# Attention exps: two of each group's 32 leave ScalarE for VectorE and GpSimd

## The reference, cut to what matters

```python
q = _rms_norm(q)
k = _rms_norm(k)
attn = jnp.einsum('bhnd,bhmd->bhnm', q, k) * scale      # scale = D ** -0.5 = 0.25
attn = jax.nn.softmax(attn, axis=-1)
y = jnp.einsum('bhnm,bhmd->bhnd', attn, v)
```

## Time and profile before

| what | us |
|---|---|
| median of 3 runs | 810.57 (808.7 to 810.73) |
| the profiled execution | 810.5 |
| its span, first to last instruction | 808.7 |
| PE busy | 781.2 (97%) |
| DVE busy | 476.2 (59%) |
| ACT busy | 523.3 (65%) |
| POOL busy | 245.1 (30%) |

### The profile page before, as it was taken

One profiled execution on the slowest core, in us unless ns is written; L12 is line 12 of the kernel. 1 busy time (PEld: TensorE's weight loads), 2 busy tenths in 40 slices (PEclk: granted clock), 3 DMA queues, 4 the chain that ended last, 5 costly groups with the idle time before them and its releaser, 6 DMA issues.

```text
span 808.7 us, 13174 instructions
## 1 busy us (share of the span) xinstructions
PE 781.2 (97%) x4440; PEld 514.7 (64%) x4440; DVE 476.2 (59%) x855; ACT 523.3 (65%) x699; POOL 245.1 (30%) x310
## 2 busy tenths in 40 slices
PE   8999999998999999999999999999999999999994
PEld 5778888886777887433332332332756788888884
DVE  5887676557866762382321211220467699999994
ACT  4432222463233226899999999999465688888883
POOL 6434444223434421500000000100000376656652
PEclk9999999999999999999999999999996999999999
DMA  8141111101132805043453432400682581111000
GB/s 247 34 80 53 41 37 52 53 1 53 42 119 100 180 2 79 1 73 109 81 143 41 79 52 28 80 1 1 219 303 104 197 303 48 56 47 43 24 12 0
DMA packets 52762, 64.99 MB, mean 80 GB/s; under 512 B 15969, under 2 KB 44009, under 8 KB 52716
## 3 DMA queue, kind: packets, MB, share of 16 engines
q1 hardware_dynamic: 44580, 55.96, 26.7%
q0 software_dynamic: 3312, 6.31, 2.5%
q10 hardware_dynamic: 4824, 2.12, 1.0%
HBM read 51.52 MB, written 15.60 MB: 83 GB/s over the span
## 4 chain that ended last, share of the span: by engine, by line
PE 83%; DVE 9%; ACT 3%; issue 2%; DMA 1%; DVEq 0%; ACTq 0%; POOLq 0%; SPq 0%
PE psum L1656 46%; PE psum L1761 15%; PE psum L1748 12%; PE psum L2033 2%; PE psum L1847 2%; DVE hl L1078 1%; DVE hh L1226 1%; PE psum L1719 1%; PE psum L1911 1%; DVE ssum L1266 1%; DMA x_tm<-in_x 1%; DVE w_lo L1527 1%; DVE parts L1335 1%; DVE parts L1334 1%; DVE qk_tm L1298 1%
## 5 line engine op out<-in xcount | busy, mean ns | idle before, releaser
L845 ACT ACTIVATE pexp<-psum 128x1024 f32<-128x1024 f32 x256 | 238.0, 1124 | 5.2 <-PE psum L1748 4.3
L832 ACT ACTIVATE hid<-psum,b_col 128x512 f32<-128x512 f32 x96 | 66.1, 689 | 164.1 <-PE psum L1656 124.1
L1761 PE MATMUL psum<-pexp,v_ones 128*32 128x512 f32 x1024 | 136.0, 604 | 0.0
L1748 PEld LDWEIGHTS psum<-q_stack,k_stack 48*128 48x128 f32 x512 | 44.3, 183 | 124.2 <-ACT pexp L845 105.2
L1748 PE MATMUL psum<-q_stack,k_stack 48*128 48x512 f32 x512 | 109.4, 476 | 2.9 <-DVE parts L1335 2.9
L1226 DVE TENSOR_SCALAR hh<-hid,scale_col 128x341 fp32r<-128x341 f32 x192 | 71.0, 411 | 61.6 <-ACT hid L832 44.4
L1078 DVE SCALAR_TENSOR_TENSOR hl<-hid,scale_col,hh 128x341 fp32r<-128x341 f32 x192 | 104.6, 586 | 3.4
L1349 DVE COPY yT<-psum 128x512 f32<-128x512 f32 x16 | 11.0, 691 | 131.4 <-PE psum L1761 131.4
L1656 PE MATMUL psum<-hh,w2h 128*128 128x512 f32 x192 | 76.8, 400 | 3.9 <-DVE hl L1078 3.8
L1656 PE MATMUL psum<-x_hi,w1h 128*128 128x512 f32 x192 | 77.4, 403 | 0.6 <-DVE x_lo L1092 0.5
L1656 PE MATMUL psum<-hh,w2l 128*128 128x512 f32 x192 | 75.4, 393 | 0.0
(11 more groups left out here) (284 smaller groups left out, 1438.0 us busy)
## 6 DMA issues: line engine op xcount, KB each, us to landing
w_all<-in_L_ffn_W SPq DMA_DIRECT2D x16, 1024.0 KB, 7.4
raw<-in_L_cond_ew SPq DMA_DIRECT2D x32, 256.0 KB, 3.3
parts_d<-parts SPq DMA_DIRECT2D x8, 1024.0 KB, 4.1
q_stack<-parts_d SPq DMA_DIRECT2D x48, 128.0 KB, 4.2
k_stack<-parts_d SPq DMA_DIRECT2D x48, 128.0 KB, 6.6
raw<-in_L_cond_sw SPq DMA_DIRECT2D x16, 256.0 KB, 3.4
x_tm<-in_x SPq DMA_DIRECT2D x4, 512.0 KB, 7.3
x_d<-x_tm SPq DMA_DIRECT2D x2, 1024.0 KB, 10.4
```

The lines of the kernel that those rows point to most:

```text
L832: act.activation(hid[k % 4][:], bank(k % 4), ACT.Gelu_apprx_tanh, bias=b1_col[:, bass.ds(4 * q + k // 2, 1)]).then_inc(gelu_done, 1)
L845: act.activation(pexp[mt % 2][:, 2 * j:2 * j + 2, 512 * h:512 * h + 512], psum[:, 2 * r:2 * r + 2, :], ACT.Exp, scale=D ** -0.5)\
L1748: ins = pe.matmul(psum[:, 2 * r + lane, :], k_stack[i][rows, j, mt * P:(mt + 1) * P], q_stack[i][rows, j, 512 * h:512 * h + 512], start=Tr ...
L1761: ins = pe.matmul(psum[VW * j:VW * j + VW, 6 + h, :], v_ones[i][:, mt, j, :], pexp[mt % 2][:, j, 512 * h:512 * h + 512], start=(mt == 0), ...
```

## The change: what it does

Units 12 and 20 of groups 1 to 7 (14 of 256 units) take another way. VectorE copies their scores from PSUM into the place in `pexp` where their exps belong. GpSimd then replaces them by `exp_base ** score`, where `exp_base` holds e to the power of 0.25, so that the result is the same exp. TensorE's `slot_free` waits for VectorE's copy where the pair held such a unit, and `values` waits for GpSimd's count beside ScalarE's. ScalarE skips these units. VectorE's loops over the groups are written out, and `split_parts` now stands in the order of the units, between the copies.

```diff
+POOL_EXPS = [(g, u) for g in range(1, 8) for u in (12, 20)]
...
+        def other_exps(n):
+            return sum(1 for g, u in POOL_EXPS if UNITS * g + u < n)
+
+        def exps_until(eng, n):
+
+            eng.wait_ge(exp_done, n - other_exps(n))
+            after(eng, pool_exp_done, other_exps(n))
...
+            pool.memset(exp_base[:], math.exp(D ** -0.5)).then_inc(exp_base_made, 1)
...
+            def exp_unit(g, u):
+
+                mt, h, j = u // HG, u % HG // 2, u % 2
+                unit = pexp[mt % 2][:, 2 * j:2 * j + 2, 512 * h:512 * h + 512]
+                pool.wait_ge(score_copied, other_exps(UNITS * g + u + 1))
+                pool.tensor_tensor(unit, exp_base[:].unsqueeze(2).to_broadcast([P, 2, 512]), unit, ALU.pow)\
+                    .then_inc(pool_exp_done, 1)
...
+                for u in range(UNITS):
+                    if g and (g, u) in POOL_EXPS:
+                        exp_unit(g, u)
...
-                if u % 2 == 0:
+                if u % 2 == 0 or (g, u - 1) in POOL_EXPS:
                     after(act, av_done, 2 * LT * g + u // 2 - 3)
...
-                    exp_unit(g, u)
+                    if (g, u) not in POOL_EXPS:
+                        exp_unit(g, u)
...
+            def copy_scores(g, u):
+
+                mt, h, j = u // HG, u % HG // 2, u % 2
+                r = pair(("scores", g, u))
+                dve.wait_ge(scored, UNITS * g + u + 1)
+                after(dve, av_done, 2 * LT * g + u // 2 - 3)
+                dve.tensor_copy(pexp[mt % 2][:, 2 * j:2 * j + 2, 512 * h:512 * h + 512],
+                                psum[:, 2 * r:2 * r + 2, :]).then_inc(score_copied, 1)
+
+            for g in range(GROUPS - 1):
+                take_output(g)
+                finish_group(g // (H // HG), g % (H // HG))
+                for u in range(UNITS):
+                    if (g + 1, u) in POOL_EXPS:
+                        copy_scores(g + 1, u)
+                    if (g + 1, u) in QK_AT:
+                        split_parts(QK_AT.index((g + 1, u)))
...
-                if what == "scores":
-                    pe.wait_ge(exp_done, UNITS * g + u + 1)
+                if what == "scores" and (g, u) in POOL_EXPS:
+                    pe.wait_ge(score_copied, other_exps(UNITS * g + u + 1))
+                elif what == "scores":
+                    pe.wait_ge(exp_done, UNITS * g + u + 1 - other_exps(UNITS * g + u))
...
-                pe.wait_ge(exp_done, UNITS * g + 2 * v + 2)
+                exps_until(pe, UNITS * g + 2 * v + 2)
```

More of the change, by code:

```diff
@@ L15 @@
+import math
 from contextlib import ExitStack
@@ L130, in layer_kernel @@
         ones = sb("ones", [P, P], F32)
+        exp_base = sb("exp_base", [P, 1], F32)
         scan_keep = sb("scan_keep", [P, RE, TT], F32)
@@ L348, in layer_kernel @@
         exp_done = sem("exp_done")
+        pool_exp_done = sem("pool_exp_done")
+        exp_base_made = sem("exp_base_made")
+        score_copied = sem("score_copied")
         av_done = sem("av_done")
@@ L700, in _ @@
                 pool.memset(v_ones[i][:, :, :, D:D + 1], 1.0).then_inc(v_base, 1)
+            def exp_unit(g, u):
[4 more added lines that the diff above has]
+                    .then_inc(pool_exp_done, 1)
+            pool.wait_ge(exp_base_made, 1)
             for g in range(GROUPS):
@@ L1833, in turn_ctx @@
                 if w == 0:
-                    pe.wait_ge(exp_done, UNITS * GROUPS)
+                    exps_until(pe, UNITS * GROUPS)
                 pe.wait_ge(ctx_done, 4 if w < 4 else 8)
```

## The result

| | median us | range of the runs | ratio to before |
|---|---|---|---|
| before | 810.57 | 808.7 to 810.73 | |
| changed | 3057.46 | 3056.78 to 3058.91 | 3.774 (3.766 to 3.783) |

The kernel is 2246.9 us slower. The forecast of 804.7 us was wrong, and the time lies far outside the range that ended at 865 us.

The account below looks back on a forecast made before the run. ScalarE's exps were taken to bound attention, with TensorE's floor next. Five groups gaining 1.2 us each, groups 1 and 2 almost nothing, gave 810.6 - 5.9 = 804.7 us, range 802.5 to 865.

Parts of the forecast that it names:

- the price of the power on GpSimd: A 128x1024 power on GpSimd was taken as under 3.5 us, from the 1.89 us product of the same shape.
- The upper bound: Longest GpSimd power considered: 14 arithmetic passes of 1.89 us, 26.5 us, making the kernel 316 us slower.
- The first rival: In attention, the GpSimd power outlasts its room, so values 6 and 10 wait: 862 us at 7.6 us a power; chance 0.42.
- The rule on operations a cycle: GpSimd bodies run about three operations a cycle: 5.7 us for a 20-operation power, making the kernel 25 us slower.
- ScalarE as the bound: In attention TensorE waits for ScalarE's exps: 32 of 0.922 us take 29.5 us, the group period.
- TensorE's floor of 28.12 us: TensorE's own pace over a plain attention group, against a period of 29.57 us; at most 1.45 us can be had.
- broken pairs: Pairs of scores on TensorE interrupted by a wait cost 0.84 us instead of 0.67; 0.25 us a group was allowed.
- groups 1 and 2 give nothing: Turned block and splits put these groups' floor at 32.5 us, period already 32.58; gain 0.1 us at most.
- The sum: Total gain over the kernel: 810.6 - 5.9 = 804.7 us, from 1.2 us in each of groups 3 to 7.
- The copy: VectorE's 128x1024 copy from PSUM takes 1.24 us, freeing the PSUM pair at no cost.
- The room of 3.5 us: Time a power may last before values 6 or 10 waits: three rounds, 4.98 us, less copy and hand-overs.
- the point from which the change is slower: Power length X where 14 stalls cancel the 6 us gain: 14 x (X - 3.5) = 6, from 3.9 us.

Follow-up runs that it names:

- one product: Changed kernel with GpSimd's power replaced by one product of the same form in groups 1 to 7, those exps not computed: 805.26 us, 0.9936 of before.
- one power: Changed kernel with a single power, unit 12 of group 4, in place of 14: 970.38 us.
- three products: Changed kernel with each GpSimd power replaced by three products, those exps not computed: 837.95 us, 1.0332 of before.
- two products: Changed kernel with each GpSimd power replaced by two products one after the other, those exps not computed: 806.02 us, 0.9950 of before.
- products in groups 3 to 7: Changed kernel with one product in place of the power and only groups 3 to 7 in the unit list: 801.98 us, 0.9905 of before.

## Why the prediction was wrong

- The step that failed is the price of the power on GpSimd: "I take a value under 3.5 us, since the row it is nearest to is the product". It is 163.2 us, 86 times the product. The row had the same engine, form and shape, but another operation, and the operation alone makes the factor of 86.
- The upper bound failed too. 14 arithmetic passes gave 26.5 us, and the power is six times that. It was built from the steps of `inverse_root`, which VectorE runs, and they say nothing of how GpSimd makes a power.
- The first rival had the mechanism: the wait for GpSimd took the place of the one for ScalarE at `values` 6 and 10, priced at 14 x (X - 3.5) - 6. With X = 163.2 this gives 2230 us, against the measured 2247. It had 0.42, and the range cut it off at X = 7.8 us. X is the term that failed. Two smaller ones were off as well and pull opposite ways: the stalls are 158.4 us in the mean and not 159.7, which takes away 18 us, and the work at the lower clock after them, which the prediction leaves out, adds some 38.
- The rule on operations a cycle from the Trainium skill, GPSIMD Engine Reference, section "Elementwise — side-by-side cycle accounting", which gave 5.7 us for a power of 20 operations (an estimate), pointed the right way but was 29 times too short. The trace does not bear it out for the power: a step takes 0.159 us, which at the 1.2 GHz that the page gives is some 190 cycles.
- ScalarE as the bound, TensorE's floor of 28.12 us and 0.25 us for broken pairs held: 28.42 us measured with one product. That groups 1 and 2 give nothing held too (32.58 us on both sides). The sum took 5.9 us where its terms give 6.0, which is of no weight. The copy, forecast at 1.24 us, took 1.225.
- The room of 3.5 us held in groups 3 to 7: one power's stall was 159.7 us, three products' 2.27. In groups 1 and 2 it was mis-sized. The prediction had the 2.2 us of the turned block in the floor of these groups, but not in their room, which is 5.7 us. So the point from which the change is slower, set at 3.9 us or a little more, lies higher: 3.5 + 5.75 / 10 = 4.1 us (an estimate, with ten stalls in place of 14). The runs show only that it is between 3.86 us, still faster than before, and 5.84.

## What to carry to other kernels

An operation on GpSimd that the trace does not show can't be priced from a row of the same shape with another operation. Where a change rests on such a price, the missing one decides, and the range has to follow the unknown, not the row. Once the bound and the next floor are known (here 29.57 and 28.12 us a group), a cheap stand-in of the same form tells whether the rest of the plan holds, and what its true operation may cost. VectorE, with 24 us a group free, could do by arithmetic what GpSimd's own instruction could not.

## What the runs showed that was not expected

- GpSimd's power of fp32 costs 0.159 us for each element of a partition, with 1, 16 or 128 partitions and with exponents of 0, 0.5 or 3 (one base, 1.284).
- With three products, stalls of 2.3 us were followed by TensorE work at the 1.2 GHz level in each of groups 3 to 7, at about 3 us a group; with two products, stalls of 0.3 to 0.4 us were not.
- A bias from SBUF on ScalarE's exp of 128x1024 from PSUM lengthens it from 0.922 to 1.013 us.
- Runs of one kernel scatter by several us (801.62 to 808.22 with products in groups 3 to 7, and 805.74 to 814.76 for the kernel before on the same chip), and the mean granted clock goes with them: 0.989 in the run of 801.62 us and 0.980 in that of 808.22, 0.994 and 0.983 in the two of the kernel before. The windows of TensorE after attention show where, in the kernel before and then in the run with one product in groups 1 to 7:

```profile
610.00:615.00 5.00, 4.00 (x17) 0.53 0.30 103
615.00:620.00 5.00, 4.94 (x18) 0.50 0.31 107
620.00:625.00 5.00, 5.00 (x13) 0.61 0.51 178
625.00:630.00 5.00, 5.00 (x37) 1.00 0.09 32
```

```profile
605.00:610.00 5.00, 4.13 (x18) 0.50 0.43 143
610.00:615.00 5.00, 5.00 (x19) 0.50 0.40 138
615.00:620.00 5.00, 5.00 (x15) 0.66 0.43 142
620.00:625.00 5.00, 5.00 (x29) 0.69 0.08 26
625.00:630.00 5.00, 5.00 (x8) 0.63 0.25 69
```

Around the routing after attention, where small products of TensorE and steps of VectorE take turns in the chain, the clock falls to the 1.2 GHz level. Before, it was back at full clock by 625 us; in this run it was still below it at 630. So a part of what attention gained was given back in this profile, 805.1 against 808.7 us of span where attention ended 7.5 us earlier (1.7 of them from before attention). Faster runs of the same kernel have a higher mean clock (0.989 in that of 802.07 us, 0.982 in the profiled one of 806.95), so it is not so in every run. What makes the clock fall there, and whether the earlier start has a part in it, was not settled.
